# Spiking feed-forward after a linear-attention scan: the last batch's tail moved between engines

## The chip, the cores and the metric

One core of one Trainium2 chip runs the whole program. The metric is the device time of one launch in microseconds (us); lower is better. Engines are named PE (TensorE), DVE (VectorE), ACT (ScalarE), POOL (GpSimd) and SP (SyncE, which issues the DMAs).

## What is computed

x is 8 batches of 512 tokens by 256 features, float32. LN is a layer norm without weights.

```python
x = x + LN(attention(LN(x)))       # 16 heads of 16; F = ret*F + coef*v k^T along time, y = (W_LTM + F) q
h = square(relu(LN(x) @ W_fc.T))   # 1024 hidden features
y = h @ W_proj.T
# five leaky steps: mem = 0.9*mem + y - reset; a spike where mem > 1
x = x + LN(number_of_spikes(y) / 5)
```

The number of spikes is a staircase in y: five thresholds (`DRIVES`, found on the host) stand for the five steps, and the count is how many of them y exceeds.

## The kernel before, in words

One batch is one round `g` of 16 slots `s`, written out by hand per engine in `iteration`. In slot `s` DVE forms two products v*k (`hebbian`, L924) and scans them along time (`scan`, L934), POOL multiplies both states by q (`read`, L1190, 128x1024), and PE adds the products of two slots into `p_y` (`sums`, L349; `sums(b, m)` waits for slots 2m and 2m+1). Other work lags: round g also does the output projection, norms and first product of the feed-forward ("up", `up`, L401: 8 blocks f of 128 hidden features; the operands are split into a high and a low part, three passes) of batch g-1, and the second product ("down", `down`, L371: 4 token tiles u, 8 blocks f each), the spike count and the last norm of batch g-2. For the count, ACT writes five sign tiles (`signs`, L679) and PE adds them with the identity (`count_spikes`, L379), so that ACT copies a count from PSUM. POOL makes the low part of the up operand (`low_x1`, L1206).

In the last round (g = 7, `after` false) batch 6's up blocks stand in slots 10 to 13 and its down tiles 0 and 1 in slots 14 and 15. Then comes the tail, in a fixed order per engine, for what is left of batch 6 (down tiles 2 and 3, its counts) and for batch 7:

- PE: the sums of slots 12 to 15, `tail_out` (L503, attention output of two token pairs), down 2, `tail_turn(0)` (L511), down 3, `tail_turn(1)`, a count, eight `tail_up` (L521), a count, then `tail_down(0..3)` (L528, 8 blocks each) with `tail_count` (L545) between.
- DVE: the last scan, statistics of batch 5's count (L888), moments and residual of the attention by pair (L1077, L1080, L1086, L1099), third norm (L1111), low part (L1117), eight `tail_square` (L1124; block n), batch 6's signs and statistics, then for each tile of batch 7 three signs (L1137), statistics, norm (L1148) and add (L1150).
- ACT: the attention copy (`copy_y`, L607), `norm4` (L602) for the batch two back, deviations (L586, L812), high parts (L825), `tail_relu` (L832), copies of down tiles (L607) and two signs of each (L840).
- POOL: `read` of slot 15, then for batches 5 and 6 the moments (L1231 to L1236), the offsets (L1241, L1242) and the add (L1201, 128x1024).
- SP stores batches 5 and 6, then one tile of batch 7 after each `tail_res` (L285).

`tail_step` makes a DVE instruction signal a semaphore and lets DVE wait for it, where the next one reads its result. `n4_done` counts the norm4 instructions, four per batch; `TILES*LAST` of it means that batch 6's are done. `down_bank[u]` are the PSUM banks of batch 7's down tiles.

Of the kernel before, what the change touches and what calls it, by code (L numbers as in the profile page):

```python
# [16 lines left out]
P = 128  # L17
# [51 lines left out]
def build(nc, x, w_qkv, w_o, w_fc, w_proj, w_ltm, head_params, shared_params, ident, head_mask, pick, out):  # L69
    ctx = ExitStack()  # L70
    with ctx:
# [6 lines left out]
        def sem(name):  # L78
# [26 lines left out]
        eps_sb = sb("eps_sb", [P, 2])  # L105
# [65 lines left out]
            tail_down tail_yf tail_sign_a tail_sign_v tail_count tail_var4 tail_dev4 tail_res tail_step rest_sign""".split()}  # L171
# [39 lines left out]
        ON_ACT = 2  # L211
# [11 lines left out]
        count_bank = [p_c[0], p_c[1], p_u[0], p_u[1]]  # L223
# [6 lines left out]
        def _(sp):  # L230
# [59 lines left out]
        def _(pe):  # L290
# [48 lines left out]
            def sums(b, m):  # L339
                half, dl = m // 4, m % 4  # L340
                if dl == 0:
                    pe.wait_ge(S["y_done"], at(2 * b + half))
                    pe.wait_ge(S["q_done"], at(2 * b + half + 1))
                    pe.matmul(p_y[:, :], wblk[:, half, :, :].rearrange("p d h -> p (d h)"), qf[:, half, :],  # L344
                              start=True, stop=False, skip_group_check=True)
                pe.wait_ge(S["prod_done"], at(SLOTS * b + 2 * m + 2))
# [45 lines left out]
            def up(b, f):  # L392
# [10 lines left out]
                last.then_inc(S["up_done"], 1)  # L403

# [127 lines left out]
            def count_rest():  # L532
                pe.wait_ge(S["rest_sign"], 1)
                pe.wait_ge(S["sign_done"], 2 * LAST)
                for j in range(STEPS):
                    last = pe.matmul(p_c[0][:, :], ident_b[:, :], sign[:, 1, j, :, :], start=(j == 0),
                                     stop=(j == STEPS - 1))
                last.then_inc(S["count_done"], 1)

            def tail_count(u):  # L540
                pe.wait_ge(S["tail_sign_a"], u + 1)
                pe.wait_ge(S["tail_sign_v"], u + 1)
                pe.wait_ge(S["spk_done"], 2 * LAST)
                for j in range(STEPS):
                    last = pe.matmul(count_bank[u][:, 0:D], ident_b[:, :], sign[:, u // 2, j, u % 2, :],  # L545
                                     start=(j == 0), stop=(j == STEPS - 1))
                last.then_inc(S["tail_count"], 1)
# [16 lines left out]
            tail_down(2)  # L564
            tail_count(1)
            tail_down(3)
            tail_count(2)
            tail_count(3)


        @block.scalar
        def _(act):
# [9 lines left out]
            def deviation(n, b):  # L582
                act.wait_ge(S[f"n{n}_var"], at(b + 1))
                if n in (1, 4):
                    eps = eps_sb[:, 1:2] if n == 4 else eps_sb[:, 0:1]
# [133 lines left out]
            def iteration(g, now, before, two_before, after):  # L719
                b, b1, b2 = g + 1, g - 1, g - 2  # L720
                for s in range(SLOTS):
# [78 lines left out]
                    if not after:  # L800
                        if s == 14: copy_yf(b1, 0)
                        if s == 15:
                            copy_yf(b1, 1)
                            signs(b1, 0)
# [3 lines left out]
            def tail_deviation(n, first, count, number):  # L808
                act.wait_ge(S[f"tail_var{n}"], number)
                tiles = slice(first, first + count)  # L810
                eps = eps_sb[:, 1:2] if n == 4 else eps_sb[:, 0:1]
# [3 lines left out]
            def rest_signs():  # L815
                act.wait_ge(S["yf_done"], TILES * LAST)
                act.wait_ge(S["count_done"], 2 * (LAST - 1))
                for j in range(ON_ACT):
                    last = nc.scalar.activation(sign[:, 1, j, :, :], yf[:, 2:4, :], ACT.Sign, bias=drive_sb[:, j:j + 1],
                                                scale=BELOW_ONE)  # L820
                last.then_inc(S["sign_done"], 1)
# [12 lines left out]
            def tail_signs(u):  # L834
                act.wait_ge(S["sign_done"], 2 * LAST)
                copy(down_bank[u][:, 0:D], yf[:, u, :], "tail_down", u + 1, "tail_yf")
                act.wait_ge(S["tail_yf"], u + 1)
                act.wait_ge(S["count_done"], 2 * LAST)
                for j in range(ON_ACT):
                    last = nc.scalar.activation(sign[:, u // 2, j, u % 2, :], yf[:, u, :], ACT.Sign,  # L840
                                                bias=drive_sb[:, j:j + 1], scale=BELOW_ONE)
                last.then_inc(S["tail_sign_a"], 1)

# [13 lines left out]
            copy_count(LAST - 1, 0)  # L857
            rest_signs()
            for n in range(2, FT):
                tail_relu(n)  # L860
            copy_count(LAST - 1, 1)
            deviation(4, LAST - 1)
            tail_signs(0)
            norm4(LAST - 1)
            tail_signs(1)
            tail_deviation(4, 0, 1, 1)
            tail_signs(2)
            tail_deviation(4, 1, 1, 2)
            tail_signs(3)
            tail_deviation(4, 2, 1, 3)  # L870
            tail_deviation(4, 3, 1, 4)
# [3 lines left out]
        def _(dve):  # L875
# [62 lines left out]
            v.memset(eps_sb[:, 1:2], LN_EPS * (2 * STEPS) ** 2)  # L938
            for j in range(STEPS):
# [186 lines left out]
            def rest_signs():  # L1126
                dve.wait_ge(S["yf_done"], TILES * LAST)
                dve.wait_ge(S["count_done"], 2 * (LAST - 1))
                for j in range(ON_ACT, STEPS):
                    last = v.tensor_scalar(sign[:, 1, j, :, :], yf[:, 2:4, :], DRIVES[j], 2.0, ALU.is_gt, ALU.mult)  # L1130
                last.then_inc(S["rest_sign"], 1)

            def tail_signs(u):
                dve.wait_ge(S["tail_yf"], u + 1)
                dve.wait_ge(S["count_done"], 2 * LAST)
                for j in range(ON_ACT, STEPS):
                    last = v.tensor_scalar(sign[:, u // 2, j, u % 2, :], yf[:, u, :], DRIVES[j], 2.0,  # L1137
                                           ALU.is_gt, ALU.mult)
                last.then_inc(S["tail_sign_v"], 1)

            def tail_spikes(u):
                dve.wait_ge(S["tail_count"], u + 1)
                dve.wait_ge(S["n4_done"], TILES * LAST)
                dve.wait_ge(S["res_done"], LAST)
                counted = count_bank[u][:, 0:D]
                tail_moments(4, u, 1, [counted])
                tail_reciprocal(4, u, 1, u + 1)
                tail_step(v.tensor_scalar(spk[:, u, :], counted, moments[3][:, u, 0:1], rdev[3][:, u:u + 1], ALU.subtract,  # L1148
                                          ALU.mult))
                v.tensor_tensor(xa[:, u, :], xa[:, u, :], spk[:, u, :], ALU.add).then_inc(  # L1150
                    S["tail_res"], 1)

            scan(LAST, SLOTS - 1, 1)
            statistics(4, LAST - 2, spk, "spk_done", 2 * (LAST - 1))
# [9 lines left out]
            tail_square(0)  # L1164
            tail_square(1)
            rest_signs()
            for n in range(2, FT):
# [4 lines left out]
            tail_signs(1)  # L1172
            tail_spikes(0)
            tail_signs(2)
            tail_spikes(1)
            tail_signs(3)
            tail_spikes(2)
            tail_spikes(3)
# [3 lines left out]
        def _(pool):  # L1182
# [153 lines left out]
```

## Time and profile before

| | us |
|---|---|
| three runs | 590.29, 593.32, 595.13 |
| their median | 593.32 |
| the profiled execution, its own time | 587.19 |
| its span, first to last instruction | 585.4 |
| outside the span (the difference) | 1.79 |

Times in rows are us from the span's start. The rounds end at about 528, where the last scan ends; the tail is the rest. In a timeline row the first number is the start, the second the stretch from there to the end of a run of like instructions; idle time and what ended it stand in brackets.

### The profile page before, as it was taken

To read this page: it belongs to the slowest core of one execution; us is meant where nothing else is said; L and a number is where in the kernel's file an instruction comes from. 1 tells how busy PE (TensorE), PEld (TensorE's weight loads), DVE (VectorE), ACT (ScalarE), POOL (GpSimd) and SP (SyncE) were. 2 spreads that over 40 slices of the span, in tenths; PEclk is the share of its full clock that TensorE was granted. 3 is DMA by queue.
4 is the path that set the end of the run, shared out by engine and by line. 5 is a ranking of instruction groups with operands and counts; after the bars stand their busy time and mean duration, and the time that the engine had idled before them with its cause. 6 is when DMAs were issued, how large, how long until landed. Compare 5 with 4: busy or idle time off the path is not lost.

```text
span 585.4 us, 7855 instructions
## 1 busy us (share of the span) xinstructions
PE 488.0 (83%) x2273; PEld 319.7 (55%) x2282; DVE 542.9 (93%) x892; ACT 313.7 (54%) x615; POOL 399.1 (68%) x274
## 2 busy tenths in 40 slices
PE   3683578559998899979997999889997999798995
PEld 2351235226575557736674657555674667466774
DVE  6799999999999999999999999999999999993647
ACT  4622322344547655577457563775567745664442
POOL 1148987686767886697868786888669776874011
PEclk9978577859999898999998998999998989999999
DMA  7475586457565649455855657473944585510102
GB/s 257 133 193 146 140 216 188 135 146 181 141 171 137 175 112 270 109 165 141 243 139 141 181 158 199 133 187 103 264 108 122 148 251 180 131 32 1 36 1 72
DMA packets 54777, 87.63 MB, mean 150 GB/s; under 512 B 5456, under 2 KB 19408, under 8 KB 54736
## 3 DMA queue, kind: packets, MB, share of 16 engines
q1 hardware_dynamic: 54160, 87.12, 54.4%
q8 instruction: 18, 0.29, 0.2%
q14 instruction: 23, 0.19, 0.1%
q10 hardware_dynamic: 576, 0.03, 0.1%
HBM read 78.74 MB, written 8.39 MB: 149 GB/s over the span
## 4 chain that ended last, share of the span: by engine, by line
PE 50%; POOL 16%; DVE 14%; issue 14%; ACT 5%; DMA 1%; ACTq 0%; DVEq 0%; POOLq 0%
PE p_c L401 13%; POOL prod L1190 11%; PE p_c L371 8%; PE p_a L305 7%; DVE state L934 7%; PE p_y L349 6%; PE p_c L362 4%; PE p_a L326 2%; POOL x1t L1206 2%; PE p_y L344 2%; POOL xt L1206 2%; DVE p_u L924 2%; PE p_u L521 1%; DVE stats L888 1%; ACT hr L663 1%
## 5 line engine op out<-in xcount | busy, mean ns | idle before, releaser
L1190 POOL TENSOR_TENSOR prod<-state,qf 128x1024 f32<-128x1024 f32 x128 | 303.4, 2372 | 94.7 <-DVE state L934 61.1
L934 DVE TENSOR_TENSOR_SCAN state<-ret,p_u 128x512 f32<-128x512 f32 x256 | 309.2, 1208 | 0.0
L924 DVE TENSOR_TENSOR p_u<-vrep,p_k 128x512 f32<-128x512 f32 x256 | 171.4, 675 | 1.8 <-ACT p_k L607 1.8
L371 PE MATMUL p_c<-wproj_sb,ht 128*128 128x256 f32 x448 | 101.9, 381 | 0.0
L305 PE MATMUL p_a<-xt,wqkv_s 128*128 128x512 f32 x276 | 85.9, 452 | 8.8 <-POOL xt L1206 3.7
L371 PEld LDWEIGHTS p_c<-wproj_sb,ht 128*128 128x128 f32 x448 | 83.7, 190 | 16.7 <-issue 5.0
L401 PE MATMUL p_c<-x1t,wfc_s 128*128 128x512 f32 x336 | 85.5, 401 | 7.6 <-POOL x1t L1206 7.6
L305 PEld LDWEIGHTS p_a<-xt,wqkv_s 128*128 128x128 f32 x276 | 55.5, 211 | 50.1 <-issue 14.5
L349 PE MATMUL p_y<-prod,summer 128*32 128x512 f32 x512 | 75.5, 666 | 6.3 <-POOL prod L1190 6.2
L401 PEld LDWEIGHTS p_c<-x1t,wfc_s 128*128 128x128 f32 x336 | 61.8, 189 | 25.7 <-POOL x1t L1206 11.5
L663 ACT ACTIVATE hr<-p_c 128x512 f32<-128x512 f32 x56 | 33.3, 594 | 25.8 <-PE p_c L401 24.0
L679 ACT ACTIVATE sign<-yf,drive_sb 128x512 bf16<-128x512 f32 x65 | 41.2, 709 | 0.2
L665 ACT ACTIVATE ht<-hr 128x512 f32<-128x512 f32 x56 | 35.4, 632 | 1.8
L362 PE MATMUL p_c<-wo_sb,yt 128*128 128x256 f32 x112 | 32.6, 457 | 0.0
L299 PE MATMUL p_a<-ident_sb,xa 128*128 128x128 f32 x64 | 12.9, 337 | 21.7 <-issue 9.7
L349 PEld LDWEIGHTS p_y<-prod,summer 128*32 128x32 f32 x512 | 10.5, 111 | 35.9 <-issue 23.5
L607 ACT COPY vf<-p_a 128x512 f32<-128x512 f32 x15 | 8.7, 582 | 39.5 <-PE p_a L305 39.3
L326 PE MATMUL p_a<-mean_sb,ksq 128*128 128x8 f32 x128 | 17.8, 266 | 13.1 <-ACT ksq L621 13.0
L1206 POOL TENSOR_TENSOR xt<-xf,xt 128x512 fp32r<-128x512 f32 x16 | 20.5, 1280 | 11.4 <-ACT xt L607 11.4
L362 PEld LDWEIGHTS p_c<-wo_sb,yt 128*128 128x128 f32 x112 | 25.5, 232 | 4.6
L326 PEld LDWEIGHTS p_a<-mean_sb,ksq 128*128 128x128 f32 x128 | 16.3, 200 | 20.3 <-ACT ksq L621 20.3
L299 PEld LDWEIGHTS p_a<-ident_sb,xa 128*128 128x128 f32 x64 | 8.6, 169 | 31.7 <-issue 20.1
(172 smaller groups left out, 568.8 us busy)
## 6 DMA issues: line engine op xcount, KB each, us to landing
vrep<-v_rows SPq DMA_DIRECT2D x256, 256.0 KB, 3.9
xa<-in_x SPq DMA_DIRECT2D x9, 512.0 KB, 5.0
v_rows<-vf SPq DMA_DIRECT2D x16, 256.0 KB, 3.1
x<-in_x SPq DMA_DIRECT2D x7, 512.0 KB, 6.7
out<-x SPq DMA_DIRECT2D x7, 512.0 KB, 3.3
ht<-in_w_fc SPq DMA_DIRECT2D x1, 1024.0 KB, 7.4
wproj_sb<-in_w_proj SPq DMA_DIRECT2D x1, 1024.0 KB, 10.3
state<-in_w_qkv SPq DMA_DIRECT2D x1, 512.0 KB, 6.1
```

The lines of the kernel that those rows point to most:

```text
L305: last = pe.matmul(bank[:, :], wqkv_s[:, i, t, first_col:first_col + P], xt[:, j, t, :], start=(t == i == j == 0), stop=(t == KT - 1 and i ...
L326: last = pe.matmul(p_a[:, u * HH:(u + 1) * HH], ksq[:, u * P:(u + 1) * P], mean_sb[:, :], start=True, stop=True)
L349: last = pe.matmul(p_y[32 * grp:32 * grp + 32, :], summer[:, half, dl, grp, :], prod[:, s % NZ, grp % 2, :], start=False, stop=(dl == 3), ...
L362: last = pe.matmul(p_c[(t + 1) % 2][:, i * D:(i + 1) * D], yt[:, half, tokens(2 * t + i)], wo_sb[:, half, :], start=(half == 0), stop=(hal ...
L371: last = pe.matmul(p_c[(u + 1) % 2][:, 0:D], ht[:, f, tokens(u)], wproj_sb[:, f, :], start=(f == 0), stop=(f == FT - 1))
L401: last = pe.matmul(p_c[(f + 1) % 2][:, :], wfc_s[:, i, t, f * P:(f + 1) * P], x1t[:, j, t, :], start=(t == i == j == 0), stop=(t == KT - 1 ...
L663: nc.scalar.activation(hr[:, f % 2, :], p_c[(f + 1) % 2][:, :], ACT.Relu).then_inc(S["relu_done"], 1)
L679: last = nc.scalar.activation(sign[:, pair, j, :, :], yf[:, 2 * pair:2 * pair + 2, :], ACT.Sign, bias=drive_sb[:, j:j + 1], scale=BELOW_ONE)
L924: v.tensor_tensor(p_u[n % NU][:, :], vrep[:, n % NV, :], p_k[:, :], ALU.mult).then_inc(S["hebb_done"], 1)
L934: v.tensor_tensor_scan(state[:, s % NS, i, :], ret[:, r:r + 1].broadcast_to([P, L]), p_u[n % NU][:, :], 0.0, ALU.mult, ALU.add).then_inc(S ...
L1190: p.tensor_tensor(prod[:, s % NZ, :, :], state[:, s % NS, :, :], qf[:, s // HS, :].unsqueeze(1).broadcast_to([P, 2, L]), ALU.mult).then_in ...
L1206: p.tensor_tensor(low, value, high.bitcast(F32), ALU.subtract).then_inc(S[done], 1)
```

## The change

1. DVE makes slot 15's product (`last_read`), not POOL; PE's last `sums` waits for it. DVE then takes the statistics.
2. Batch 6's down tile 1 goes from slot 15 behind both `tail_out`; down 2 and 3 move back one place each, and so do ACT's copies of tiles 1 to 3. The five signs of tiles 0 and 1 on ACT, 3 and 2 sign instructions of batch 6's other pair, and both counting groups on PE go.
3. DVE counts spikes instead: a `tensor_scalar` (is_gt) and four chained `scalar_tensor_tensor` (is_gt, add). For batch 6 on 128x512, SBUF to SBUF (`count_rest`): pair 0 ahead of the squares, pair 1 one instruction behind each of the first five squares. For batch 7 on 128x256 straight from the PSUM bank into `yf` (`tail_count`). ACT's copies of batch 7's down tiles and its signs go, as do PE's `tail_count`.
4. `tail_down` waits for its hidden block f row by row, not for all eight.
5. The first two up blocks of batch 6 take the high passes before they wait for the low part (`up_first_pair`).
6. The count is no longer doubled, so a third eps value is set. The last add of batch 7's tiles 0 to 2 is made by POOL (`tail_sum`), that of tile 3 stays on DVE; the norm of a tile writes `yf` in place.

Cut to its core:

```diff
             for u in range(TILES):
-                sp.wait_ge(S["tail_res"], u + 1)
+                if u < TILES - 1:
+                    sp.wait_ge(S["tail_sum"], u + 1)
+                else:
+                    sp.wait_ge(S["tail_res"], 1)
...
+                if b == LAST and m == HS - 1:
+                    pe.wait_ge(S["prod_done"], SLOTS * B - 1)
+                    pe.wait_ge(S["tail_prod"], 1)
...
+            def up_first_pair(b):
+                for f in range(2):
+                    pe.wait_ge(S["relu_done"], at(FT * b + f - 1))
...
+                    for t in range(KT):
+                        pe.wait_ge(S["x1t_high"], KT * b + t + 1)
+                        for i in range(2):
+                            pe.matmul(p_c[(f + 1) % 2][:, :], wfc_s[:, i, t, f * P:(f + 1) * P], x1t[:, 0, t, :],
+                                      start=(t == i == 0), stop=False)
+                pe.wait_ge(S["x1t_low"], KT * (b + 1))
+                for f in range(2):
+                    for t in range(KT):
+                        last = pe.matmul(p_c[(f + 1) % 2][:, :], wfc_s[:, 0, t, f * P:(f + 1) * P], x1t[:, 1, t, :],
+                                         start=False, stop=(t == KT - 1))
+                    last.then_inc(S["up_done"], 1)
...
-                        if 10 <= s < 14:
+                        if s == 10: up_first_pair(b1)
+                        if 11 <= s < 14:
...
-                        if s == 15: down(b1, 1, False)
...
             def tail_down(u):
-                pe.wait_ge(S["tail_h"], FT)
                 for f in range(FT):
+                    pe.wait_ge(S["tail_h"], f + 1)
...
             tail_out(0)
             tail_out(1)
+            down(LAST - 1, 1, False)
+            tail_turn(0)
             down(LAST - 1, 2, False)
-            tail_turn(0)
+            tail_turn(1)
             down(LAST - 1, 3, False)
-            tail_turn(1)
-            count_spikes(LAST - 1, 0)
             for f in range(FT):
                 tail_up(f)
-            count_rest()
-            tail_down(0)
-            tail_down(1)
-            tail_count(0)
-            tail_down(2)
-            tail_count(1)
-            tail_down(3)
-            tail_count(2)
-            tail_count(3)
+            for u in range(TILES):
+                tail_down(u)
...
             tail_deviation(2, 2, 2, 2)
-            copy_yf(LAST - 1, 2)
+            copy_yf(LAST - 1, 1)
             tail_high(0)
             tail_deviation(3, 2, 2, 2)
+            copy_yf(LAST - 1, 2)
+            tail_high(1)
             copy_yf(LAST - 1, 3)
-            tail_high(1)
-            for n in range(2):
+            for n in range(FT):
                 tail_relu(n)
...
             deviation(4, LAST - 1)
-            tail_signs(0)
             norm4(LAST - 1)
...
+            def last_read():
+                dve.wait_ge(S["state_done"], 2 * SLOTS * B)
+                dve.wait_ge(S["sum_done"], HS * LAST + HS - 2)
+                dve.wait_ge(S["q_done"], 2 * B)
+                s = SLOTS - 1
+                v.tensor_tensor(prod[:, s % NZ, :, :], state[:, s % NS, :, :],
+                                qf[:, s // HS, :].unsqueeze(1).broadcast_to([P, 2, L]), ALU.mult).then_inc(
+                    S["tail_prod"], 1)
+
+            def count_rest(pair, j):
+                tiles = slice(2 * pair, 2 * pair + 2)
+                if j == 0:
+                    dve.wait_ge(S["yf_done"], TILES * (LAST - 1) + 2 * (pair + 1))
+                    dve.wait_ge(S["res_done"], LAST - 1)
+                    tail_step(v.tensor_scalar(spk[:, tiles, :], yf[:, tiles, :], DRIVES[0], None, ALU.is_gt))
+                    return
+                last = v.scalar_tensor_tensor(spk[:, tiles, :], yf[:, tiles, :], DRIVES[j], spk[:, tiles, :], ALU.is_gt,
+                                              ALU.add)
...
+            def tail_count(u):
+                dve.wait_ge(S["tail_down"], u + 1)
+                drive = down_bank[u][:, 0:D]
+                tail_step(v.tensor_scalar(yf[:, u, :], drive, DRIVES[0], None, ALU.is_gt))
+                for j in range(1, STEPS):
+                    tail_step(v.scalar_tensor_tensor(yf[:, u, :], drive, DRIVES[j], yf[:, u, :], ALU.is_gt, ALU.add))
 
             def tail_spikes(u):
-                dve.wait_ge(S["tail_count"], u + 1)
                 dve.wait_ge(S["n4_done"], TILES * LAST)
...
+                tail_moments(4, u, 1, [yf[:, u, :]])
                 tail_reciprocal(4, u, 1, u + 1)
...
             scan(LAST, SLOTS - 1, 1)
+            last_read()
             statistics(4, LAST - 2, spk, "spk_done", 2 * (LAST - 1))
...
-            tail_square(0)
-            tail_square(1)
-            rest_signs()
-            for n in range(2, FT):
+            for j in range(STEPS):
+                count_rest(0, j)
+            for n in range(FT):
                 tail_square(n)
+                if n < STEPS: count_rest(1, n)
             statistics(4, LAST - 1, spk, "spk_done", 2 * LAST)
-            tail_signs(0)
+            tail_count(0)
             scales(4, LAST - 1)
-            tail_signs(1)
             tail_spikes(0)
-            tail_signs(2)
-            tail_spikes(1)
-            tail_signs(3)
-            tail_spikes(2)
-            tail_spikes(3)
+            for u in range(1, TILES):
+                tail_count(u)
+                tail_spikes(u)
...
-            read(LAST, SLOTS - 1)
...
+            for u in range(TILES - 1):
+                pool.wait_ge(S["tail_norm4"], u + 1)
+                p.tensor_tensor(xa[:, u, :], xa[:, u, :], yf[:, u, :], ALU.add).then_inc(S["tail_sum"], 1)
```

## Rows read from the trace of the kernel before

**Rows 1.** Busy time of each engine, from the page: us (share of the span) xinstructions.

```profile
PE 488.0 (83%) x2273; PEld 319.7 (55%) x2282; DVE 542.9 (93%) x892; ACT 313.7 (54%) x615; POOL 399.1 (68%) x274
```

**Rows 2.** The costliest DVE group, from the page: xcount | busy, mean ns | idle before it.

```profile
L934 DVE TENSOR_TENSOR_SCAN state<-ret,p_u 128x512 f32<-128x512 f32 x256 | 309.2, 1208 | 0.0
```

**Rows 3.** Timeline, 505 to 533: low part, first up blocks, down tiles 0 and 1.

```profile
507.13 2.48 POOL L1206 TENSOR_TENSOR x1t<-x1f,x1t 128x512 fp32r<-128x512 f32 x2
...
509.67 5.85 PE L401 MATMUL p_c<-x1t,wfc_s 128*128 128x512 f32 x24 [2.96 <-POOL x1t L1206]
...
525.19 7.07 PE L371 MATMUL p_c<-wproj_sb,ht 128*128 128x256 f32 x32
```

**Rows 4.** Timeline, 525 to 540: end of the last round and start of the tail.

```profile
525.72 2.32 DVE L934 TENSOR_TENSOR_SCAN state<-ret,p_u 128x512 f32<-128x512 f32 x2
...
528.12 2.36 POOL L1190 TENSOR_TENSOR prod<-state,qf 128x1024 f32<-128x1024 f32 x1 [0.47 <-DVE state L934]
...
532.19 1.93 PE L349 MATMUL p_y<-prod,summer 128*32 128x512 f32 x16
...
532.76 3.17 ACT L679 ACTIVATE sign<-yf,drive_sb 128x512 bf16<-128x512 f32 x5
...
535.83 0.56 ACT L607 COPY yt<-p_y 128x512 f32<-128x512 f32 x1
...
536.45 3.72 PE L503 MATMUL p_u<-wo_sb,yt 128*128 128x256 f32 x16 [2.33 <-ACT yt L607]
```

**Rows 5.** Groups of DVE by line and shape: xcount | busy us, mean ns | idle before.

```profile
L1099 DVE SCALAR_TENSOR_TENSOR xa<-p_u,rdev,xa 128x256 f32<-128x256 f32 x4 | 1.8, 479 | 0.1
...
L988 DVE TENSOR_TENSOR state<-state,p_u 128x1024 f32<-128x1024 f32 x1 | 1.2, 1220 | 0.0
...
L1111 DVE TENSOR_SCALAR oo<-xa,rdev 128x256 f32<-128x256 f32 x4 | 1.2, 350 | 0.1
...
L1148 DVE TENSOR_SCALAR spk<-p_u,moments,rdev 128x256 f32<-128x256 f32 x2 | 1.1, 544 | 0.1
```

**Rows 6.** Timeline, 539 to 552: attention norm to the first up block of batch 7.

```profile
539.56 0.30 ACT L812 ACTIVATE dev<-moments,eps_sb 128x2 f32<-128x2 f32 x1
...
543.79 0.66 PE L511 MATMUL p_a<-ident_sb,oo 128*128 128x128 f32 x4 [0.17 <-DVE oo L1111]
...
544.28 3.62 PE L371 MATMUL p_c<-wproj_sb,ht 128*128 128x256 f32 x16
...
549.74 1.66 PE L521 MATMUL p_u<-x1t,wfc_s 128*128 128x512 f32 x6 [0.32 <-DVE x1t L1117]
```

**Rows 7.** Timeline, 561 to 573: last square, batch 6's norm, first down tiles.

```profile
561.86 0.69 DVE L1124 TENSOR_TENSOR ht<-p_u,hr 128x512 f32<-128x512 f32 x1 [0.70 <-ACT hr L832]
...
562.61 3.72 PE L528 MATMUL p_a<-wproj_sb,ht 128*128 128x256 f32 x16 [0.32 <-DVE ht L1124]
...
563.00 1.41 DVE L888 BATCH_NORM_STATS2 stats<-spk 128x6 f32<-128x256 f32 x4 [0.45 <-ACT spk L607]
...
565.86 0.30 ACT L586 ACTIVATE dev<-squares,eps_sb 128x4 f32<-128x4 f32 x1 [2.89 <-POOL squares L1236]
...
567.44 0.17 DVE L901 RECIPROCAL rdev<-dev 128x4 f32<-128x4 f32 x1
...
568.20 2.07 ACT L602 ACTIVATE spk<-spk,nmr,rdev 128x256 f32<-128x256 f32 x4 [0.47 <-POOL nmr L1242]
...
570.35 2.35 POOL L1201 TENSOR_TENSOR x<-x,spk 128x1024 f32<-128x1024 f32 x1 [2.19 <-ACT spk L602]
```

**Rows 8.** Timeline of DVE alone, 570.6 to 572.6: one sign instruction.

```profile
570.56 2.29 DVE L1137 TENSOR_SCALAR sign<-yf 128x256 bf16<-128x256 f32 x1 [2.95 <-ACT yf L607]
```

**Rows 9.** Timeline, 579 to 584: the last tile.

```profile
581.02 0.42 DVE L1077 BATCH_NORM_STATS2 stats<-p_u 128x6 f32<-128x256 f32 x1
...
582.22 0.54 DVE L1148 TENSOR_SCALAR spk<-p_u,moments,rdev 128x256 f32<-128x256 f32 x1
...
582.80 0.42 DVE L1150 TENSOR_TENSOR xa<-xa,spk 128x256 f32<-128x256 f32 x1
```

More of the change, by code:

```diff
@@ L104, in build @@
         summer = sb("summer", [P, HALVES, 4, GRP, 4 * HH])
-        eps_sb = sb("eps_sb", [P, 2])
+        eps_sb = sb("eps_sb", [P, 3])
         ksum = sb("ksum", [P, KT, H])
@@ L170, in build @@
             tail_out tail_x1 tail_var2 tail_dev2 tail_var3 tail_dev3 tail_n3 tail_turned tail_high tail_low tail_up tail_relu tail_h
-            tail_down tail_yf tail_sign_a tail_sign_v tail_count tail_var4 tail_dev4 tail_res tail_step rest_sign""".split()}
+            tail_down tail_prod tail_var4 tail_dev4 tail_norm4 tail_sum tail_res tail_step""".split()}
         v_in = [sem(f"v_in{i}") for i in range(NV)]
@@ L345, in sums @@
                               start=True, stop=False, skip_group_check=True)
-                pe.wait_ge(S["prod_done"], at(SLOTS * b + 2 * m + 2))
+                if b == LAST and m == HS - 1:
+                    pe.wait_ge(S["prod_done"], SLOTS * B - 1)
+                    pe.wait_ge(S["tail_prod"], 1)
+                else:
+                    pe.wait_ge(S["prod_done"], at(SLOTS * b + 2 * m + 2))
                 for grp in range(GRP):
@@ L403, in up @@
                 last.then_inc(S["up_done"], 1)
+            def up_first_pair(b):
+                for f in range(2):
+                    pe.wait_ge(S["relu_done"], at(FT * b + f - 1))
+                    if f == 1:
+                        pe.wait_ge(S["yf_done"], TILES * b)
+                    else:
+                        pe.wait_ge(S["spk_done"], 2 * (b - 1) + 1)
+                    for t in range(KT):
[9 more added lines that the diff above has]
+                    last.then_inc(S["up_done"], 1)
             def count_last():
@@ L530, in tail_down @@
                 last.then_inc(S["tail_down"], 1)
[L532 to L547, printed above, removed]
             sums(LAST, 6)
@@ L584, in deviation @@
                 if n in (1, 4):
[L585 removed]
+                    eps = eps_sb[:, 0:1] if n == 1 else eps_sb[:, 2:3] if b == LAST - 1 else eps_sb[:, 1:2]
                     nc.scalar.activation(dev[n - 1][:, :], squares[n][:, :], ACT.Sqrt, bias=eps, scale=1.0 / D).then_inc(
@@ L800, in iteration @@
                     if not after:
[L801 to L804, printed above, removed]
+                        if s == 15: copy_yf(b1, 0)
             run(iteration)
@@ L810, in tail_deviation @@
                 tiles = slice(first, first + count)
-                eps = eps_sb[:, 1:2] if n == 4 else eps_sb[:, 0:1]
+                eps = eps_sb[:, 2:3] if n == 4 else eps_sb[:, 0:1]
                 nc.scalar.activation(dev[n - 1][:, tiles], moments[n - 1][:, tiles, 1], ACT.Sqrt, bias=eps).then_inc(
                     S[f"tail_dev{n}"], 1)
[L815 to L821, printed above, removed]
             def tail_high(pair):
@@ L832, in tail_relu @@
                 nc.scalar.activation(hr[:, n % 2, :], up_bank[n % 4][:, :], ACT.Relu).then_inc(S["tail_relu"], 1)
[L834 to L842, printed above, removed]
             copy_y(LAST, 1)
@@ L849, in _ @@
             tail_deviation(2, 2, 2, 2)
-            copy_yf(LAST - 1, 2)
+            copy_yf(LAST - 1, 1)
             tail_high(0)
             tail_deviation(3, 2, 2, 2)
+            copy_yf(LAST - 1, 2)
+            tail_high(1)
             copy_yf(LAST - 1, 3)
-            tail_high(1)
-            for n in range(2):
+            for n in range(FT):
                 tail_relu(n)
-            copy_count(LAST - 1, 0)
-            rest_signs()
-            for n in range(2, FT):
-                tail_relu(n)
-            copy_count(LAST - 1, 1)
             deviation(4, LAST - 1)
-            tail_signs(0)
             norm4(LAST - 1)
-            tail_signs(1)
-            tail_deviation(4, 0, 1, 1)
-            tail_signs(2)
-            tail_deviation(4, 1, 1, 2)
-            tail_signs(3)
-            tail_deviation(4, 2, 1, 3)
-            tail_deviation(4, 3, 1, 4)
+            for u in range(TILES):
+                tail_deviation(4, u, 1, u + 1)
         @block.vector
@@ L938, in _ @@
             v.memset(eps_sb[:, 1:2], LN_EPS * (2 * STEPS) ** 2)
+            v.memset(eps_sb[:, 2:3], LN_EPS * STEPS ** 2)
             for j in range(STEPS):
@@ L1124, in tail_square @@
                 v.tensor_tensor(ht[:, n, :], up_bank[n % 4][:, :], hr[:, n % 2, :], ALU.mult).then_inc(S["tail_h"], 1)
[L1126 to L1139, printed above, removed]
+            def last_read():
[6 more added lines that the diff above has]
+                    S["tail_prod"], 1)
@@ new lines, in count_rest @@
+            def count_rest(pair, j):
[7 more added lines that the diff above has]
+                                              ALU.add)
+                if j < STEPS - 1:
+                    tail_step(last)
+                else:
+                    last.then_inc(S["spk_done"], 1)
@@ L1145, in tail_spikes @@
-                counted = count_bank[u][:, 0:D]
-                tail_moments(4, u, 1, [counted])
+                tail_moments(4, u, 1, [yf[:, u, :]])
                 tail_reciprocal(4, u, 1, u + 1)
[L1148 to L1151, printed above, removed]
+                last = v.tensor_scalar(yf[:, u, :], yf[:, u, :], moments[3][:, u, 0:1], rdev[3][:, u:u + 1], ALU.subtract,
+                                       ALU.mult)
@@ L1153, in _ @@
+                if u < TILES - 1:
+                    last.then_inc(S["tail_norm4"], 1)
+                else:
+                    tail_step(last)
+                    v.tensor_tensor(xa[:, u, :], xa[:, u, :], yf[:, u, :], ALU.add).then_inc(S["tail_res"], 1)
             scan(LAST, SLOTS - 1, 1)
+            last_read()
             statistics(4, LAST - 2, spk, "spk_done", 2 * (LAST - 1))
```

8 lines of the change are left out of this document (removed).

## The prediction, made before the changed kernel was run

> **What bounds the kernel now.** I read the page's engine shares first, then its costliest groups, then the timeline of the last 60 us, and the row that ends the span last. DVE is busy 93% of the span [rows 1], and its scans never wait [rows 2]: through the rounds DVE sets the pace. No edit there takes an instruction from DVE, so the rounds should end where they do now, with the last scan at 525.72 + 2.32 = 528.04 [rows 4]. What can change is the tail: 528.04 to the end of the last add at 582.80 + 0.42 = 583.22 [rows 9], plus 585.4 - 583.22 = 2.18 for the last store. I follow the changed tail in the clock of the profiled execution (own time 587.19, span 585.4, 1.79 outside); the median of the runs, 593.32, is 1.010 times as long, and I scale by that at the end.
>
> **Prices.** A DVE instruction that takes one column a cycle costs 0.42 us for 256 columns (the add, [rows 9]), 0.69 for 512 (the square, [rows 7]) and 1.22 for 1024 (L988, [rows 5]): 1.04 ns a column and 0.16 fixed. The new `scalar_tensor_tensor` with constants has no row. Nearest is L1099, the same operation at 256 columns out of PSUM with a scalar per partition, 0.48; the add, two tensors and no scalar, is 0.42. The upper end is L1148 with two such scalars, 0.544 [rows 5]; the lower end is the 0.35 of L1111. I take 0.43, near the add, since constants need no fetch. Chained instructions begin some 0.03 after the end of the one before (a gap that the last tile shows between its steps: 582.22 + 0.54 to 582.80 is 0.04). One count of a batch 7 tile is so 5 x 0.46 = 2.3 us, on 512 columns 0.43 (below) + 4 x 0.73 = 3.35 us.
>
> **Part 5, high passes first.** The first up block waits 2.96 us until POOL's low part is done [rows 3]. Of 12 passes of two blocks 8 go into that wait; 4 are left behind 509.6, at 5.85/24 = 0.24 each, so both blocks are done near 510.6 instead of 509.67 + 12 x 0.24 = 512.6: 2 us sooner. Down tile 0 then ends near 526.7 instead of 525.19 + 3.5 = 528.7. What waits next is PE's last `sums`, and that needs the last product (next part), so nearly all of this is hidden. Without it, the sums of slots 12 and 13 would end at 528.7 + 1.0 and those of 14 and 15 at 530.7, against 530.25 below: this part is worth 0 to 0.5 us, and as the third stretch shows, less at the end.
>
> **Parts 1 and 2, until the attention output.** DVE makes the last product in 1.22 (L988's shape) right behind the scan: 528.04 to 529.28; POOL needed 528.12 to 530.48. POOL's slot 14 product is through before 528.12, so they don't meet. The sums of two slots take 1.93/2 = 0.97: 530.25. Today down tile 1 stands in front of them (they begin at 532.19), and then the five signs hold ACT from 532.76 until its `copy_y` at 535.83 [rows 4]. Both are gone: `copy_y` 530.3 to 530.9, `tail_out` at 530.95 instead of 536.45. That is 5.5 us early.
> Less of it arrives. DVE's statistics of batch 5 now stand behind the product, and start at 529.25. From there to the deviation took 2.86 (563.00 to 565.86), from the reciprocal to norm4 0.76 (567.44 to 568.20), norm4 itself 2.07 [rows 7]. So deviation 532.1, reciprocal 532.45, norm4 533.2 to 535.3. ACT's first attention deviation is queued behind norm4. By the shift alone it would come 539.56 - 536.45 = 3.1 behind `tail_out` [rows 4, 6], at 534.05; it comes at 535.3. The shift falls from 5.5 to 4.25.
>
> **Down tiles 1 to 3, until batch 7's first up block.** PE now has three down tiles here instead of two and no count. `tail_out` ends at about 534.5; down 1 (7.07/2 = 3.5 [rows 3]) to 538.0; `tail_turn(0)` waits for the norm, 543.79 - 4.25 = 539.55; down 2 begins 0.5 later (543.79 to 544.28 [rows 6]), 540.05 to 543.6; turn 1 and 0.5 more; down 3 from 544.1 to 547.65. The low part is ready by 549.7 - 4.25 = 545.4, so PE's own queue is late: first up block 547.65 instead of 549.74. The shift is 2.1. DVE's count of pair 0 (3.35 from about 545.5, to 548.9) hides ahead of the first square, which needs the first up block and its relu, 1.66 + 0.65 behind 547.65 [rows 6]. The count of pair 1 puts 0.69 + 0.03 behind each of five squares of 0.69: 1.41 against 1.46 (5.85/4) that PE takes for a block. That just fits; if each were 0.1 longer than the block, up to 0.5 us would be lost, less what three bare squares catch up.
>
> **Parts 3, 4 and 6, the last stretch.** The last square ends 2.1 early, at 562.55 - 2.1 = 560.45. Down tile 0 need not wait for it: it starts when the last up block leaves PE, near 558.9 (562.61 - 2.1 = 560.5 with the old wait [rows 7]; the last row's block needs relu and square, 1.5 after 558.9, but stands 7 x 0.44 = 3.1 behind the start), and ends at 562.4. PE would then deliver a tile every 3.5: 562.4, 565.9, 569.4, 572.9. It is not PE that ends this any more:
> - count of tile 0: 562.4 to 564.7. `scales` of batch 6 is queued behind it on DVE, though its deviation (statistics at 560.45, + 2.86, + 0.3) is ready at 563.6. Reciprocal 564.7, norm4 565.45 to 567.55.
> - `tail_spikes(0)` waits for `n4_done`, all of norm4: DVE idles from 564.9 to 567.55. From its statistics to the norm took 582.22 - 581.02 = 1.20 [rows 9]: the norm is due at 568.75.
> - POOL's add of batch 6 starts with the same signal, 567.6, and takes 2.35 [rows 7], to 569.95. The sign instruction that DVE issued at 570.56, while this add ran from 570.35 to 572.70, took 2.29 until 572.85 [rows 8]; it is of the tensor_scalar kind, SBUF to SBUF, like the norm of the changed kernel, which no longer reads PSUM. I take it that the norm is held too: it ends at 570.15 instead of 569.15. This costs 1.0; its other end is 0.
> - tiles 1 and 2: count 2.3, 1.20 to the norm, 0.4 for it: 3.9 each, more than PE's 3.5. Tile 1's norm ends at 574.05, tile 2's at 577.95. POOL's adds of a tile, 2.35/4 = 0.6, lie beside the next count and cost nothing.
> - tile 3: count to 580.25, norm from 581.45 to 581.85, add 581.9 to 582.3.
> The last add ends at 582.3 instead of 583.22: 0.9 us sooner, of 5.5 gained at the start. Own time 587.19 - 0.9 = 586.3; times 593.32/587.19, 592.4.
>
> **A rule weighed.** At 256 columns SBUF to SBUF L1111 takes 0.35, which is less than the 0.42 of one column a cycle even with its scalar, and the held row has a bf16 output, not f32. The Trainium skill, VectorE: DVE Perf Modes, section "Mode 2×_2P — use both read ports for one tensor", says that an f32 tensor_scalar within SBUF also takes both read ports, and GPSIMD Engine Reference (section 1) that these contend with GpSimd. By that the f32 norm is held like the bf16 sign (586.3); by a reading of the row that binds the hold to bf16 it would be 585.3. The trace has no f32 case.
>
> **The rivals.**
> A, the forecast: DVE bound, hold and waits as above, 586.3 (592.4). Its own range is 585.5 to 587.
> B, semaphore waits between chained instructions cost DVE nothing and they overlap as unchained ones do. L1111's pair would begin 0.26 apart; taking 0.09 off the 0.43 makes a count 1.7, tile 3.3, below PE's 3.5. The norms then end at 570.15 (held all the same), 573.4, 576.7 and the last add near 580.4: 2.8 sooner, 584.4 (590.5). For it: independent ones do overlap; against it: the steps of the last tile show no overlap [rows 9]. The Trainium skill (VectorE: DVE Perf Modes, "The DRAIN you can't avoid") has a rule to this effect, that the semaphore after each costs nothing extra; the rows of the last tile speak against it.
> C, slower: the counting instruction costs what L1148 does, 0.544, because reading PSUM and SBUF together and two operations in one cost more. All 20 of batch 7 are on the path, counts 1 to 3 for DVE and count 0 through `scales` and norm4: 20 x 0.114 = 2.3 more, end 584.6, 588.6 (594.7). It decides from 0.9/20 = 0.045 more each, at 0.475, which is L1099's own price.
> D, PE bound: if the counts fitted beside PE, down 3 at 572.9, count 2.3, then 1.20 + 0.4 + 0.47 to the last add at 577.3: 5.9 sooner, 581.3 (587.3). Against it: 3.9 a tile is DVE's alone.
> E, the shift of 2.1 is not reached, as DVE falls behind in the squares or PE's three down tiles meet another wait: each 1 us there is 1 us at the end, 587.3 (593.4).
>
> **Chances and range.** A 0.55, B (or no hold) 0.17, C 0.14, D 0.05, E 0.09. No case but D comes near 1%, and 1% is about what a measurement of this kernel can tell from no change. Faster by over 1%: D and a part of B with the spread of the runs, 0.05; slower by over 1%, C with that spread, 0.03; within 1%, 0.92. The cases span 587.3 to 594.7; the runs before lie 3.0 below and 1.8 above their median, a median of three less. From B less half that spread to C with some: 588.8 to 595.2.
>
> **What would show it.** Right: last product on DVE at 1.2 us; `tail_out` near 531; first attention deviation right behind norm4; first tail up block near 547.7; DVE idle some 2.7 us before tile 0's statistics; tile 0's norm stretched until POOL's add ends; tiles 3.9 apart while PE idles at the end. Wrong: an is_gt/add instruction far from 0.43, squares lagging the relus, a last scan away from 528, or DVE waiting for `tail_down` at tiles 1 to 3.

## The result, and where the time went

Over 11 runs each on one chip the changed kernel took 589.67 us (median; 586.37 to 590.31), the kernel before 591.76 (588.08 to 595.13). The ratio of the runs is 0.9934, 95% interval 0.9908 to 0.9960: 2.4 to 5.4 us faster. The forecast, 0.9 us of 587, was in the right direction and four times too small.

The first reading misleads. The changed kernel's profiled execution has a span of 588.0, longer than the 585.4 of the one before. So I split both executions at the end of the last scan, and call what follows, up to the end of the last add, the tail.

| execution | last scan ends | last add ends | tail |
|---|---|---|---|
| before | 528.04 | 583.22 | 55.18 |
| changed | 532.25 | 585.87 | 53.62 |

The rounds of this execution ended 4.2 us later, and its first scan already began 3.0 later (35.1 against 32.1). The tail is 1.56 shorter. That is more than forecast (0.92) and still less than the runs measured. The experiments look for the rest.

The stretch at the start of the tail, timeline of the changed kernel (start, length, engine, line; the first row is batch 6's down tile 0, still in the last round):

```profile
529.26 3.62 PE L376 MATMUL p_c<-wproj_sb,ht 128*128 128x256 f32 x16
...
532.28 1.23 DVE L1101 TENSOR_TENSOR prod<-state,qf 128x1024 f32<-128x1024 f32 x1
...
534.86 0.58 ACT L607 COPY yt<-p_y 128x512 f32<-128x512 f32 x1 [1.23 <-PE p_y L354]
...
535.49 3.72 PE L527 MATMUL p_u<-wo_sb,yt 128*128 128x256 f32 x16 [0.76 <-ACT yt L607]
...
537.39 2.08 ACT L602 ACTIVATE spk<-spk,nmr,rdev 128x256 f32<-128x256 f32 x4 [0.80 <-POOL nmr L1225]
...
539.37 0.28 ACT L809 ACTIVATE dev<-moments,eps_sb 128x2 f32<-128x2 f32 x1
...
551.24 1.74 PE L545 MATMUL p_u<-x1t,wfc_s 128*128 128x512 f32 x6
```

Read each against the end of the last scan. `tail_out` (L527) starts 3.24 behind it, where it was 8.41 [rows 4]: 5.2 us won. The first attention deviation (L809) comes right behind norm4 (L602), at 7.12 instead of 11.52 [rows 6]: 4.4 left. The first up block of batch 7 (L545) starts at 18.99 instead of 21.70: 2.7 left. The last stretch takes more of it:

```profile
563.44 0.69 DVE L1094 TENSOR_TENSOR ht<-p_u,hr 128x512 f32<-128x512 f32 x1 [0.70 <-ACT hr L821]
...
566.26 0.42 DVE L1122 TENSOR_SCALAR yf<-p_a 128x256 f32<-128x256 f32 x1 [0.82 <-PE p_a L552]
...
566.72 1.80 DVE L1124 SCALAR_TENSOR_TENSOR yf<-p_a,yf 128x256 f32<-128x256 f32 x4
...
568.55 0.18 DVE L870 RECIPROCAL rdev<-dev 128x4 f32<-128x4 f32 x1
...
569.32 2.07 ACT L602 ACTIVATE spk<-spk,nmr,rdev 128x256 f32<-128x256 f32 x4 [2.12 <-POOL nmr L1225]
...
571.42 0.43 DVE L1047 BATCH_NORM_STATS2 stats<-yf 128x6 f32<-128x256 f32 x1 [2.69 <-ACT spk L602]
571.47 2.35 POOL L1184 TENSOR_TENSOR x<-x,spk 128x1024 f32<-128x1024 f32 x1 [2.18 <-ACT spk L602]
...
572.63 1.34 DVE L1130 TENSOR_SCALAR yf<-yf,moments,rdev 128x256 f32<-128x256 f32 x1
...
577.37 0.41 DVE L1130 TENSOR_SCALAR yf<-yf,moments,rdev 128x256 f32<-128x256 f32 x1
...
585.45 0.42 DVE L1136 TENSOR_TENSOR xa<-xa,yf 128x256 f32<-128x256 f32 x1
```

The count of tile 0 (L1122, L1124) takes 2.26; the reciprocal of batch 6 is queued behind it, norm4 behind that, and DVE idles 2.69 us for norm4. Then POOL's add (L1184) starts, and the norm of tile 0 takes 1.34 where that of tile 1 takes 0.41. The norms of the tiles end 3.81 apart, while PE finished its last down tile at 576.6.

### The profile page after: what moved, and what is told of

Read it like the earlier page. It is cut to its first block, busy times and chain, and to the rows that moved or that the text cites. A ratio compares the mean times of both kernels' runs of the same rounds, so it can differ in the third digit from the quotient of the medians.

```text
span 588.0 us, 7778 instructions
## 1 busy us (share of the span) xinstructions
PE 491.8 (84%) x2252; PEld 322.3 (55%) x2252; DVE 552.1 (94%) x906; ACT 303.3 (52%) x594; POOL 399.0 (68%) x276
## 4 chain that ended last, share of the span: by engine, by line
PE 45%; DVE 21%; issue 15%; POOL 12%; ACT 5%; DMA 1%; ACTq 0%; DVEq 0%; POOLq 0%
DVE state L903 12%; PE p_c L406 11%; PE p_c L376 10%; POOL prod L1173 8%; PE p_a L306 6%; PE p_y L354 5%; PE p_c L367 4%; PE p_a L327 2%; DVE p_u L893 2%; POOL x1t L1189 2%; PE p_y L345 2%; PE p_u L545 1%; POOL xt L1189 1%; DVE stats L857 1%; ACT hr L663 1%
## 5 line engine op out<-in xcount | busy, mean ns | idle before, releaser
L306 PE MATMUL p_a<-xt,wqkv_s 128*128 128x512 f32 x276 | 88.0, 460 | 6.6 <-POOL xt L1189 2.6
L406 PE MATMUL p_c<-x1t,wfc_s 128*128 128x512 f32 x324 | 84.1, 406 | 4.5 <-POOL x1t L1189 4.5
L306 PEld LDWEIGHTS p_a<-xt,wqkv_s 128*128 128x128 f32 x276 | 56.9, 217 | 48.0 <-issue 15.1
L406 PEld LDWEIGHTS p_c<-x1t,wfc_s 128*128 128x128 f32 x324 | 60.3, 191 | 22.0 <-POOL x1t L1189 7.3
L679 ACT ACTIVATE sign<-yf,drive_sb 128x512 bf16<-128x512 f32 x60 | 38.1, 710 | 0.2
L327 PE MATMUL p_a<-mean_sb,ksq 128*128 128x8 f32 x128 | 19.4, 278 | 12.9 <-ACT ksq L621 12.9
L327 PEld LDWEIGHTS p_a<-mean_sb,ksq 128*128 128x128 f32 x128 | 18.0, 217 | 20.5 <-ACT ksq L621 20.5
```

What stands on the lines that cost most here:

```text
L306: last = pe.matmul(bank[:, :], wqkv_s[:, i, t, first_col:first_col + P], xt[:, j, t, :], start=(t == i == j == 0), stop=(t == KT - 1 and i ...
L327: last = pe.matmul(p_a[:, u * HH:(u + 1) * HH], ksq[:, u * P:(u + 1) * P], mean_sb[:, :], start=True, stop=True)
L406: last = pe.matmul(p_c[(f + 1) % 2][:, :], wfc_s[:, i, t, f * P:(f + 1) * P], x1t[:, j, t, :], start=(t == i == j == 0), stop=(t == KT - 1 ...
L679: last = nc.scalar.activation(sign[:, pair, j, :, :], yf[:, 2 * pair:2 * pair + 2, :], ACT.Sign, bias=drive_sb[:, j:j + 1], scale=BELOW_ONE)
```

## The experiments

All tails below are measured as above, from one profile each; the same kernel gave 53.62 and 53.66. Where ratios stand, they come from several rounds against the kernel before on the same chip.

**The two kernels again.** Two theories stood for the 2 us that the tails of the first two profiles did not show.

> The kernel before, unchanged, timed against itself. In the profiled executions the tail (end of the last scan to end of the last add) is 55.18 us before and 53.62 after the change, 1.56 shorter, while the measured ratio of 0.9934 stands for 3.9 us. Theory T (the tail is all that changed, the rest is scatter of the rounds): ratio 1.000 within some 0.3%, tail 55.2 within 0.2, and the last scan ends anywhere from 527 to 533. Theory H (the changed kernel's rounds are shorter too): the end of the last scan is the same in every profile of one kernel within 0.5 us.

> The changed kernel, unchanged. T: ratio 0.9973 (1.56 of 590), tail 53.6 within 0.2. H: ratio 0.993 again and a last scan that ends earlier than in the kernel before.

The kernel before against itself: ratio 1.002 (1.0001 to 1.0039), so a ratio of this kind can be off by some 0.2%. Its tail was not 55.2 but **56.73**. The changed kernel: 0.9940 (0.9916 to 0.9963), tail 53.66. So the tail of the changed kernel repeats, that of the kernel before does not. Theory T had the tail of the kernel before wrong, and with it the ratio of the changed kernel (0.9973, outside the interval); theory H had that ratio, but not its claim that the last scan of one kernel ends within 0.5 us: 528.04 and 532.96 for the same kernel. What differs is seen in batch 6's first up blocks. In the repeat of the kernel before (timeline):

```profile
514.58 7.41 PE L401 MATMUL p_c<-x1t,wfc_s 128*128 128x512 f32 x24 [4.06 <-POOL x1t L1206]
...
531.66 7.07 PE L371 MATMUL p_c<-wproj_sb,ht 128*128 128x256 f32 x32
```

They start 18.38 ahead of the end of the last scan, in the first profile 18.37, but 24 of them take 7.41 us instead of 5.85 [rows 3], and down tile 0 starts 1.30 ahead of that end instead of 2.85. The busy times in stretches of 2 us (us of stretch, then PE, PEld, DVE, ACT, POOL with counts, the granted PE clock, DMA share, GB/s) show why. First profile of the kernel before:

```profile
508.00:510.00 2.00, 0.33 (x1) 0.30 (x2) 2.00 (x4) 2.00 (x4) 2.00 (x3) 1.00 0.68 132
510.00:512.00 2.00, 2.00 (x10) 1.64 (x9) 2.00 (x3) 0.73 (x3) 2.00 (x2) 1.00 0.62 154
512.00:514.00 2.00, 2.00 (x11) 1.59 (x10) 2.00 (x4) 1.83 (x4) 2.00 (x1) 1.00 0.67 125
```

Its repeat:

```profile
512.00:514.00 2.00, 0.00 (x0) 0.00 (x0) 2.00 (x3) 1.93 (x4) 2.00 (x3) 1.00 0.63 156
514.00:516.00 2.00, 1.42 (x4) 1.13 (x5) 2.00 (x3) 0.00 (x0) 2.00 (x2) 0.67 0.65 218
516.00:518.00 2.00, 2.00 (x6) 1.60 (x5) 2.00 (x3) 0.53 (x1) 2.00 (x2) 0.50 0.41 134
518.00:520.00 2.00, 2.00 (x10) 1.54 (x9) 2.00 (x4) 1.43 (x4) 1.24 (x2) 0.97 0.36 131
```

PE had stood still for 4.06 us, waiting for the low part, and then got a clock of 0.50, which is 1.2 GHz, for some 3 us. In the first profile the wait was 2.96 and the clock stayed at 1.00, 2.4 GHz. The changed kernel had the fall too (0.56 and 0.59 in the stretches 514 to 518 of its profile), so it is not that the change avoids it.

**Does the tail follow the clock?**

> The kernel before once more, for the profile alone. In one of its two profiles TensorE's clock fell to 1.2 GHz for some 3 us at the start of batch 6's up blocks, 24 of them took 7.41 us instead of 5.85, and the tail was 56.73 instead of 55.18. If the tail of this kernel follows that clock: tail 56.7 with the fall, 55.2 without. If the 1.55 has another cause: a tail that does not go with the clock.

The same kernel, with nothing edited. The wait was 4.05 us, the clock fell to 0.50 and 0.67 (516 to 520), the 24 passes took 7.40 and the tail was 56.71. In three profiles of the kernel before the tail is 56.7 with the fall, twice, and 55.2 without, once. The whole tail shifts with it: `tail_out`, the first deviation and the first up block of batch 7 each come 1.5 us later against the last scan in the two than in the one. Against 56.7 the changed kernel's 53.65 is 3.1 us shorter, a ratio of 0.9948, inside both intervals. The forecast was computed from the one execution of the three in which the kernel before was at its best.

**Where the change hides it: the high passes.** The changed kernel without part 5:

```diff
-                        if s == 10: up_first_pair(b1)
-                        if 11 <= s < 14:
+                        if 10 <= s < 14:
```

> The changed kernel with the first two up blocks as before (the low part waited for first). PE's down tile 0 would end 2.2 us behind the last scan with the fall of the clock, the last sums 4.1, tail_out would start at 4.8 instead of 3.24, and the first attention deviation 0.75 later: tail 54.4 (53.9 without the fall). If ACT's norm4 hid it: 53.6. If all of the high passes' gain reached the end: 55.6.

Tail 54.61, with the clock at 0.50 again, so part 5 is worth 0.97 here, from one profile. `tail_out` started 4.93 behind the last scan instead of 3.24, and the first deviation 8.05 instead of 7.12. The other 0.7 is hidden by norm4 in front of it, as the expectation had it. The kernel before with part 5 alone:

```diff
+                        if s == 10: up_first_pair(b1)
-                        if 10 <= s < 14:
+                        if 11 <= s < 14:
```

> The kernel before with part 5 alone (high passes of the first two up blocks ahead of the wait). PE is on its path in the last round: down tiles 0 and 1, the last sums, ACT's signs. Theory P (PE's lateness there is paid in full by the kernel before): tail 56.7 - 1.7 to 2.0 = 54.7 to 55.0 with the fall of the clock, 53.3 without it, ratio 0.997. The forecast's view (the wait of the sums is the product's): in this kernel, where down tile 1 stands in front of the sums, it gives the same; if neither holds, tail 56.7.

Ratio 0.9965 (0.9932 to 0.9998), but in the profile the tail is 56.37, only 0.35 shorter. The first half of theory P held: down tile 0 started 2.98 ahead of the end of the last scan instead of 1.30, and ACT's attention copy came 1.68 sooner against it. Then it was lost in a place that neither expectation named. In stretches of 1 us (columns as above):

```profile
540.00:541.00 1.00, 0.00 (x0) 0.00 (x0) 0.00 (x0) 1.00 (x2) 0.00 (x0) 1.00 0.00 0
541.00:542.00 1.00, 0.00 (x0) 0.00 (x0) 0.00 (x0) 1.00 (x3) 0.00 (x0) 1.00 0.00 0
...
543.00:544.00 1.00, 1.00 (x5) 0.77 (x5) 0.00 (x0) 0.76 (x2) 0.20 (x1) 0.69 0.00 0
544.00:545.00 1.00, 1.00 (x4) 0.81 (x3) 0.00 (x0) 1.00 (x3) 0.00 (x0) 0.50 0.00 0
545.00:546.00 1.00, 1.00 (x4) 0.81 (x3) 0.89 (x4) 0.31 (x1) 0.61 (x1) 0.50 0.00 0
546.00:547.00 1.00, 1.00 (x4) 0.78 (x4) 0.54 (x4) 0.29 (x1) 1.00 (x1) 0.60 0.00 0
```

PE stood for 2.33 us behind ACT's signs, as in the kernel before [rows 4], and this time the clock fell behind it: `tail_out` took 5.41 us instead of 3.72. The three profiles of the kernel before have the same wait and no fall. With the signs gone (part 2) the changed kernel has no such wait: PE idles 0.76 there, and no profile of it shows a fall in the tail up to the last down tile. The ratio of 0.9965 stands for more than the 0.35 of this one profile; whether other executions go without the second fall is not shown.

**What the chain of the last stretch costs.** Own statistics buffers for batch 7 (stats, moments, dev, rdev), so that tile 0 no longer waits for norm4:

```diff
-                dve.wait_ge(S["n4_done"], TILES * LAST)
-                tail_moments(4, u, 1, [yf[:, u, :]])
+                tail_moments(5, u, 1, [yf[:, u, :]])
...
-            norm4(LAST - 1)
-            for u in range(TILES):
-                tail_deviation(4, u, 1, u + 1)
+            tail_deviation(5, 0, 1, 1)
+            norm4(LAST - 1)
+            for u in range(1, TILES):
+                tail_deviation(5, u, 1, u + 1)
```

> The changed kernel with statistics buffers of their own for batch 7, so that tail_spikes(0) no longer waits for norm4 of batch 6, and ACT's deviation of tile 0 ahead of that norm4. If the wait for n4_done is on the path (it left DVE idle for 2.7 us, and the add of POOL behind it held the norm for 0.9): tail 53.6 - 2.7 - 0.9 = 50.0 to 50.3. If PE's down tiles set the end instead: no change below 53.4.

Tail 50.00; ratio 0.9920 (0.9893 to 0.9947). By the profile, the wait and the hold behind it (a DVE instruction that does not end until POOL's add has) were 3.6 us of the changed kernel's tail. The time does not confirm that size: the changed kernel's ratio of the same rounds is 0.9940, only 1.2 us away with overlapping intervals, and the tail alone (56.7 to 50.0) would give 0.9887, just under the interval. Two pieces follow, each alone, from the changed kernel: the hold, and the part of the wait that DVE's queue order makes. POOL's big add behind the small one of tile 0:

```diff
-                add_feed_forward(b)
+                if b == LAST - 2: add_feed_forward(b)
...
+                if u == 1: add_feed_forward(LAST - 1)
                 pool.wait_ge(S["tail_norm4"], u + 1)
```

> The changed kernel with POOL's add of batch 6 behind its add of tile 0, so that POOL stands still while DVE norms tile 0. If that add held the norm (1.34 us instead of 0.41): the norm takes 0.41 and the tail is 0.93 shorter, 52.7. If the 1.34 has another cause (norm4's or the scalars' reads): it stays, tail 53.6.

The norm of tile 0, timeline of DVE:

```profile
572.18 0.41 DVE L1130 TENSOR_SCALAR yf<-yf,moments,rdev 128x256 f32<-128x256 f32 x1
```

0.41, and the tail is 52.72. The add did hold it. The scales ahead of the count:

```diff
+            scales(4, LAST - 1)
             tail_count(0)
-            scales(4, LAST - 1)
```

> The changed kernel with the scales of batch 6 ahead of the count of tile 0 on DVE. The deviation is ready 0.9 us after the down tile, so the count starts 0.9 later, but norm4 is issued 1.4 earlier and the count (2.3) still ends before norm4 does: tail 1.4 shorter, 52.2. If DVE's queue order is not what delays norm4: tail 53.6 or 0.9 longer, 54.5.

Tail 52.32, 1.3 shorter. The queue order on DVE delays norm4.

**Parts 1 and 4, each undone alone in the changed kernel.**

```diff
-            last_read()
+            read(LAST, SLOTS - 1)          # on POOL
```

> The changed kernel with slot 15's product on POOL again. The sums come 1.2 us later, tail_out too. If norm4 of batch 5 in ACT's queue binds the first attention deviation: POOL's moments end at about the same time as now, and the tail is only 0.4 longer, 54.0. If the sums bind: 1.2 longer, 54.8.

```diff
+                pe.wait_ge(S["tail_h"], FT)
                 for f in range(FT):
-                    pe.wait_ge(S["tail_h"], f + 1)
```

> The changed kernel where down tiles of batch 7 wait for all eight blocks again. Down tile 0 then starts when the last square ends, 1.5 us later; count, scales and norm4 hang on it: tail 55.1. If DVE were bound there by something else (statistics of batch 6 in front of the count end 0.8 before the down tile): only the part beyond its cover, less than 1.5.

Tails 53.98 and 55.33. The product on DVE is worth 0.35 of the 1.08 by which `tail_out` starts sooner: norm4 of batch 5 binds behind it. The wait row by row is worth 1.7, the most of the three parts that were undone alone (1, 4 and 5). Parts 2, 3 and 6 were not.

**A version that beats both.** On top of the statistics buffers of their own, cut to its core; `count_first(u)` is the first is_gt of tile u alone:

```diff
-            norm4(LAST - 2)
             tail_deviation(2, 0, 2, 1)
+            norm4(LAST - 2)
...
+                    if u == 0 and j == 1: scales(4, LAST - 1)
...
                 tail_moments(5, u, 1, [yf[:, u, :]])
+                if 1 <= u < TILES - 1: count_first(u + 1)
...
+                if u == 2: add_feed_forward(LAST - 1)
                 pool.wait_ge(S["tail_norm4"], u + 1)
```

> As own_stats, and: norm4 of batch 5 behind the first attention deviation on ACT (0.8 us at the first deviation), scales of batch 6 inside the count of tile 0, the first is_gt of tiles 2 and 3 in the wait for ACT's deviation of the tile before, POOL's add of batch 6 behind its add of tile 1. Expected tail 50.2 - 0.8 - 0.7 = 48.7; if the first deviation is not on the path 49.5; ratio to the kernel before (55.2 - 48.7)/590 off, 0.989.

Ratio 0.9838 (0.9813 to 0.9864), tail 49.33. The tail was hoped to be 48.7, and by itself would give 0.9875, just above the interval. With norm4 moved, the first deviation came at 6.36 instead of 7.12 behind the last scan, but the third norm of the first pair took 1.54 us for two instructions, 0.62 in the changed kernel, with POOL's add of batch 5 now beside it:

```profile
539.27 2.35 POOL L1191 TENSOR_TENSOR x<-x,spk 128x1024 f32<-128x1024 f32 x1 [3.59 <-ACT spk L602]
...
540.49 1.54 DVE L1082 TENSOR_SCALAR oo<-xa,rdev 128x256 f32<-128x256 f32 x2
```

```diff
                 if b == LAST - 2:
+                    pool.wait_ge(S["tail_n3"], 1)
                     add_feed_forward(b)
```

> best1 with POOL's add of batch 5 held back until the third norm of the first pair is done. In best1 that norm (two tensor_scalar, f32, SBUF to SBUF) took 1.54 us instead of 0.62, with the add of 2.35 running since 1.2 us before it. If the add held it: 0.62, and the tail is 0.9 shorter, 48.4. If not: 49.3.

```profile
539.85 0.61 DVE L1082 TENSOR_SCALAR oo<-xa,rdev 128x256 f32<-128x256 f32 x2
...
540.54 2.37 POOL L1191 TENSOR_TENSOR x<-x,spk 128x1024 f32<-128x1024 f32 x1 [5.51 <-DVE oo L1082]
```

Tail 48.43, as expected; ratio 0.9868 (0.9833 to 0.9904). The two were timed on different chips and their intervals overlap, so the time does not say which is faster; the profiles do, by 0.9, and show the third norm at 0.61 again. By tails the two are 7.4 and 8.3 us faster than the kernel before with its fall, by ratios 9.6 and 7.8.

## Why the prediction was right or wrong

- **The time of the kernel before: wrong, and the largest part of the miss.** The step is the first one, "528.04 to the end of the last add", 55.18, taken as the tail to be improved. Two of three profiles give 56.7. The forecast scaled the execution's time to the median of the runs as if it were slow everywhere alike (1.010). It is not: 1.5 us of the difference sit in one place, batch 6's up blocks at half clock, and the kernel before pays them in full through down tile 1, the sums and the signs. I had argued that PE's lateness in the last round is hidden after the change, which is just why the change gains when PE is late, and didn't draw that.
- **Part 5, "worth 0 to 0.5 us, and less at the end": mis-sized.** It is 0.97 in the changed kernel with the clock down; the sum was made at full clock. Its first step, PE's down tile 0 done 2 us sooner, did not come about against the execution that it was computed from: the tile starts 2.99 ahead of the end of the last scan instead of 2.85, because the passes behind the wait ran at half clock. Against the two executions with the fall (1.30) it is 1.7. What waits instead, norm4, was named rightly.
- **Parts 1 and 2: right.** `tail_out` at 3.24 behind the scan (2.91 forecast), deviation right behind norm4 at 7.12 (7.26).
- **Three down tiles before the up blocks: mis-sized.** 19.61 behind the scan was forecast, 18.99 measured. The first turn came 0.18 sooner than forecast (11.33 instead of 11.51), and I gave each tile 3.55 and each turn 0.5: down tile 2 takes 3.45 until the second turn, that turn 0.44, and down tile 3 3.27 until the up block. The gain there is 2.7, not 2.1. Of the 0.62, 0.35 is left at the count of tile 0 (34.01 behind the scan, 34.36 forecast).
- **The end bound by DVE: right in kind.** Count 2.26 (2.3), idle time before tile 0's statistics 2.69 (2.7), tiles 3.81 apart (3.9). The last difference, over three tiles, is 0.3; with the 0.35 it makes up the 0.6 by which the tail came shorter than forecast.
- **The hold: right, and now shown for f32.** 1.34 instead of 0.41. The Trainium skill (VectorE: DVE Perf Modes, "Mode 2×_2P — use both read ports for one tensor") has f32 tensor_scalar in that mode, and the Trainium skill (GPSIMD Engine Reference, "1. Specifications") has its contention with GpSimd; the traces agree, twice (the norm of tile 0, 0.41 again in `add_behind`, and the third norm, 0.61 for two again in `best2`). The count, with one tensor in PSUM, ran beside POOL's adds of a tile at the same 0.46 a step as without them.
- **Rival B, waits free:** down. A chained step starts 0.46 behind the one before (four take 1.80, each 0.42); the first is_gt of tile 2, which needs nothing of the norm of tile 1 in front of it, starts 0.33 behind that norm of 0.41 (577.37 and 577.70), and independent norms of 0.35 start 0.27 apart. The Trainium skill's sentence that the semaphore costs nothing (VectorE: DVE Perf Modes, "The DRAIN you can't avoid") does not describe these rows. **Rival C:** down, no counting instruction of batch 7 took more than 0.46 with its wait. **D and E:** DVE was the bound, and the shift was larger, not smaller.

In all the tail was forecast at 54.26 and came at 53.62: 0.6 of the miss is in the changed kernel, 1.5 in the kernel before. The rest up to the 3.5 to 3.9 us of the ratios lies within their intervals. The rounds did not become shorter: the last scan ended at 532.2 on average in four profiles of kernels with the old tail (528.0 to 534.0) and at 532.1 in ten with the new one (529.9 to 535.4). Most of that scatter lies ahead of the first scan, which begins between 32.1 and 36.9; from there to the end of the last scan it is 497.1 to 498.5 in thirteen profiles and 496.0 in the first profile of the kernel before, which was at its best there too. What makes either scatter is open. The clock is partly open: it fell after all waits of 4.05 to 4.07 us (three profiles), not after that of 2.96, but after 2.03 in the changed kernel and in every other with part 5, and after 2.33 ahead of `tail_out` in one profile of four. Open, too, is whether the changed kernel would gain from an execution without the fall, since each of its profiles had it.

## What to carry to other kernels

Before summing a gain of 1 us from one profile, find out whether that execution is a typical one: look for the stretch where the granted clock fell or could have fallen, and ask whether its engine is on the path before and after the change. A change that takes an engine off the path also takes that engine's bad moments off it. And when a wait goes or an instruction moves, check which SBUF-to-SBUF tensor_scalar of DVE will then stand beside a long GpSimd instruction; putting the latter off gave 0.9 us of tail twice.

## What the runs showed of the hardware

- PE's wait ahead of batch 6's up blocks, 2.03 to 4.07 us, was followed by about 3 us at 1.2 GHz in thirteen of fourteen profiles, and not in the one with 2.96. The wait of 2.33 ahead of `tail_out` was followed by it in one of four. 24 up passes took 7.41 instead of 5.85 us, `tail_out` 5.41 instead of 3.72.
- An f32 tensor_scalar of 128x256 within SBUF, 0.41 us, took 1.34 (changed kernel) and 1.27 (`scales_first`) when it was issued 1.2 us after a 2.35 us add of GpSimd began, and ended 0.15 behind it. Statistics, reciprocals and a scalar_tensor_tensor that reads PSUM were not held.
